# Seven pairs and two single tiles in layer 1: four weight sums read from PSUM while the weight pieces are transposed

## The reference

```python
# layer 0
W  = L0_cond_weights[itok]                      # (32, 64, 64), one 64x64 matrix per batch entry
y  = einsum('bct,bcd->bdt', x, W)
T  = where(abs(w) < 0.05, 0, sign(w)) * mean(abs(w), axis=0)
x  = x + y @ T + b                              # 1024 x 1024
# layer 1
y  = einsum('bct,bcd->bdt', x, L1_cond_weights[itok])
w  = NF4_LEVELS[q_weight] * q_scale             # (1024 out, 1024 in), scale per group of 64
x  = x + y @ w.T + bias + 4 * (y @ lora_A.T) @ lora_B.T
```

## Time and profile before

| what | value |
|---|---|
| time, median of three runs | 360.85 us (360.42 to 361.82) |
| time of the profiled execution | 360.83 us |
| its span, first to last instruction | 359.0 us |
| outside the span | 1.83 us |
| mean granted TensorE clock | 0.998 |
| PE busy | 352.2 us, 98% of the span |

### The profile page before, as it was taken

One profiled execution on the slowest core, in us unless ns is written; L12 is line 12 of the kernel. 1 busy time (PEld: TensorE's weight loads), 2 busy tenths in 40 slices (PEclk: granted clock), 3 DMA queues, 4 the chain that ended last, 5 costly groups with the idle time before them and its releaser, 6 DMA issues.

```text
span 359.0 us, 5496 instructions
## 1 busy us (share of the span) xinstructions
PE 352.2 (98%) x1832; PEld 298.7 (83%) x1832; DVE 242.0 (67%) x363; ACT 161.1 (45%) x285; POOL 224.7 (63%) x146
## 2 busy tenths in 40 slices
PE   8899999999999999999999999999999999999996
PEld 8768788888888888888888888888888888888884
DVE  5789969896996899873899979355262452634523
ACT  2787467776886877752232314213041130321300
POOL 0488999986976888876520220866366663666632
PEclk9999999999999999999999999999999999999999
DMA  6894411953345245333311330304215032150202
GB/s 235 289 328 138 151 31 30 339 203 115 134 168 181 88 156 203 125 120 121 108 76 62 123 118 3 120 0 155 88 63 181 1 140 103 60 182 2 117 31 88
DMA packets 27838, 44.63 MB, mean 124 GB/s; under 512 B 8834, under 2 KB 17026, under 8 KB 27810
## 3 DMA queue, kind: packets, MB, share of 16 engines
q1 hardware_dynamic: 26242, 43.67, 35.0%
q10 hardware_dynamic: 1568, 0.61, 0.7%
HBM read 27.49 MB, written 16.78 MB: 123 GB/s over the span
## 4 chain that ended last, share of the span: by engine, by line
PE 87%; DVE 3%; POOL 2%; issue 2%; ACT 2%; SPq 1%; DMA 1%; POOLq 0%; DVEq 0%; ACTq 0%
PE acc L1157 33%; PE acc L1195 32%; PE xT L1121 10%; PE acc L1137 6%; PE spare L1121 3%; POOL col_scale L596 2%; PE acc L1222 2%; DMA w_in<-in_L_ffn_w 1%; PE acc L1224 1%; DVE hl L872 1%; PE xT L1204 1%; DVE W L925 1%; ACT hh L684 0%; SPq L428 0%; SPq L426 0%
## 5 line engine op out<-in xcount | busy, mean ns | idle before, releaser
L569 POOL TENSOR_TENSOR X<-X,bias 128x1024 f32<-128x1024 f32 x28 | 67.5, 2412 | 29.3 <-PE xT L1121 29.1
L1157 PE MATMUL acc<-T,hh 128*128 128x512 f32 x192 | 76.0, 396 | 0.0
L1157 PE MATMUL acc<-T,hl 128*128 128x512 f32 x192 | 75.0, 391 | 0.0
L723 ACT ACTIVATE spare<-q_raw 128x512 f32<-128x512 int32 x96 | 56.0, 598 | 19.1 <-DVE side_p L913 5.1
L1195 PE MATMUL acc<-W,hh 128*128 128x512 f32 x192 | 61.1, 389 | 0.0
L1021 DVE TENSOR_TENSOR X<-X,acc 128x512 f32<-128x512 f32 x36 | 24.8, 688 | 34.8 <-PE acc L1195 18.6
L1121 PEld LDWEIGHTS xT<-mix,X 128*128 128x128 f32 x352 | 42.7, 192 | 1.5
L1121 PE MATMUL xT<-mix,X 128*128 128x128 f32 x352 | 42.8, 275 | 0.0
L1195 PEld LDWEIGHTS acc<-W,hh 128*128 128x128 f32 x192 | 36.0, 188 | 7.5
L1157 PEld LDWEIGHTS acc<-T,hl 128*128 128x128 f32 x192 | 36.1, 188 | 7.4
L628 POOL TENSOR_TENSOR X<-X,ys 128x512 f32<-128x512 f32 x18 | 22.6, 1286 | 31.1 <-DVE ys L1010 31.1
(11 more groups left out here) (98 smaller groups left out, 662.0 us busy)
## 6 DMA issues: line engine op xcount, KB each, us to landing
out<-X SPq DMA_DIRECT2D x26, 512.0 KB, 3.0
X<-out SPq DMA_DIRECT2D x16, 512.0 KB, 3.4
X<-in_x SPq DMA_DIRECT2D x12, 512.0 KB, 3.4
q_raw<-in_L_ffn_q_weight SPq DMA_DIRECT2D x16, 256.0 KB, 3.0
w_in<-in_L_ffn_w SPq DMA_DIRECT2D x14, 256.0 KB, 6.5
x_first<-in_x SPq DMA_DIRECT2D x4, 512.0 KB, 4.6
out<-x_first SPq DMA_DIRECT2D x4, 512.0 KB, 6.8
out<-X SPq DMA_DIRECT2D x4, 256.0 KB, 2.0
```

The costliest lines, as they stand in the source:

```text
L569: pool.tensor_tensor(x_of(g), x_of(g), (bias1 if g >= NT else bias)[:, :], ALU.add).then_inc(s_xb, 1)
L723: act.activation(dst, q_raw[:, d % QS, :, :].rearrange("p o i -> p (o i)"), ACT.Copy, scale=slope, bias=offset).then_inc(s_line, 1)
L1157: mm = pe.matmul(acc[:, bank_of(q), :], a[:, k, :], b, start=(k == 0 and j == 0), stop=(k == KB - 1 and j == len(terms) - 1))
```

## The change

Layer 1 has two single tiles (16 and 17) and seven pairs. The four sums are no longer made from stored high and low parts. ACT copies a B11 and a B12 piece as they are in PSUM (`keep_block`) ahead of its `high_w`; DVE makes T1, then T3 and T2, then T4 from the bank `wT` and the kept tiles (`sums_with`, one instruction for each sum), directly behind `low_w`. PE's next `turn_w` waits for these too. Pieces except those with `r = 1` are transposed one slot later. The high and low parts of the 16 sums (`high_sum`, `low_sum`: 16 instructions on ACT and 16 on DVE) are made in slots 32 to 35, and the weight tiles lie in another order so that the kept tiles fit. `lines_by` replaces the even share of ACT's lines: in every slot it takes at least the lines that the maxima of the same slot need.

```diff
-    SB = NT + 4
+    SB = NT + 2
-    W_ORDER = (T1, T2, B11, B21, B22, T3, B12)
+    W_ORDER = [(B11, 1), (B12, 1), (B21, 1), (B22, 1), (B11, 0), (B12, 0), (B21, 0), (B22, 0),
+               (T1, 0), (T1, 1), (T2, 0), (T2, 1), (T3, 0), (T3, 1)]
-    NTS = 12
-    COMPLETE = ((T1, 3), (T3, 5), (T2, 6), (T4, 10))
+    SPLIT = (T4, T1, T3, T2)
+    NTS = len(SPLIT)
+    SUMS_BY = (0, 4, 8, 12, NTS * HB)
+    def lines_by(m):
+        done = share(2 * NC * ND, m)
+        if done == 0:
+            return 0
+        d, c = divmod(done - 1, 2 * NC)
+        sign, j = divmod(c, NC)
+        return max(share(2 * NL * ND, m), 2 * NL * d + NL * sign + j + 2)
     def sums_by(m):
-        return NTS * HB * (m - NH * NT) // (NH * (SB - NT))
+        return SUMS_BY[m - NH * NT]
     def turned_in(d):
-        return max(NH * F, ready_in(d) + 2)
+        return max(NH * F, ready_in(d) + 2) + (d % 4 != 1)
...
+            def keep_block(d):
+                j, r = divmod(d, 4)
+                act.wait_ge(s_wT, d + 1)
+                act.activation(as_is((T2, T3)[r], j), wT_flat, ACT.Copy).then_inc(s_asis, 1)
+            def high_sum(u):
+                j, i = divmod(u, NTS)
+                c = SPLIT[i]
+                act.wait_ge(s_made, NTS * HB)
+                if u == 0:
+                    act.wait_ge(s_acc, NH * NT)
+                if c == T2:
+                    act.wait_ge(s_Tl, NTS * j + SPLIT.index(T4) + 1)
+                act.activation(w1(0, c, j), as_is(c, j), ACT.Copy).then_inc(s_Th, 1)
...
                         if turned_in(d) == m - 1:
+                            if d % 4 < 2:
+                                keep_block(d)
                             high_w(d)
...
-                        lines(share(per, m), share(per, m + 1))
+                        lines(lines_by(m), lines_by(m + 1))
...
+            def sums_with(d):
+                j, r = divmod(d, 4)
+                if r == 1:
+                    dve.wait_ge(s_asis, 2 * j + 1)
+                    dve.tensor_tensor(as_is(T1, j), wT_flat, as_is(T2, j), ALU.subtract).then_inc(s_made, 1)
+                elif r == 2:
+                    dve.wait_ge(s_asis, 2 * j + 2)
+                    dve.tensor_tensor(as_is(T3, j), wT_flat, as_is(T3, j), ALU.subtract).then_inc(s_made, 1)
+                    dve.wait_ge(s_made, NTS * j + 1)
+                    dve.tensor_tensor(as_is(T2, j), wT_flat, as_is(T1, j), ALU.subtract).then_inc(s_made, 1)
+                elif r == 3:
+                    dve.wait_ge(s_made, NTS * j + 3)
+                    dve.tensor_tensor(as_is(T4, j), wT_flat, as_is(T2, j), ALU.subtract).then_inc(s_made, 1)
+            def low_sum(u):
+                j, i = divmod(u, NTS)
+                c = SPLIT[i]
+                dve.wait_ge(s_Th, u + 1)
+                dve.tensor_tensor(w1(1, c, j), as_is(c, j), w1(0, c, j).bitcast(F32), ALU.subtract
+                                  ).then_inc(s_Tl, 1)
...
                         if turned_in(d) == m - 1:
                             low_w(d)
+                            sums_with(d)
...
                 if c in SPLIT:
+                    pe.wait_ge(s_Tl, NTS * (HB - 1) + SPLIT.index(c) + 1)
...
                 need(pe, s_Wl, d)
+                need(pe, s_made, NTS * (d // 4) + (0, 0, 1, 3)[d % 4])
```

More of the change, by code:

```diff
@@ L249, in build @@
             x_first = sb("x_first", [P, F, T], F32, first_use)
-        W01 = sb("W01", [P, NPR, 2, HB // 2, BANK], F32R)
+        with ExitStack() as second_use:
+            W01_sums = sb("W01_sums", [P, 2 * NPR, 2, BANK], F32, second_use)
+        W01 = sb("W01", [P, 2 * NPR, 2, BANK], F32R)
         with ExitStack() as first_use:
@@ L257, in build @@
             b_wide = sb("b_wide", [P, KB, P], F32, first_use)
-        W23 = sb("W23", [P, NPR, 2, HB // 2, BANK], F32R)
+        with ExitStack() as second_use:
+            W23_sums = sb("W23_sums", [P, 2 * NPR, 2, BANK], F32, second_use)
+        W23 = sb("W23", [P, 2 * NPR, 2, BANK], F32R)
         def w1(part, c, j):
@@ L263, in w1 @@
                 return W_T4[:, part, j, :]
-            return (W01, W23)[j // 2][:, W_ORDER.index(c), part, j % 2, :]
+            return (W01, W23)[j // 2][:, W_ORDER.index((c, j % 2)), part, :]
         def w_raw(k, n):
@@ L380, in build @@
         s_res1 = sem("s_res1")
-        s_T = sem("s_T")
+        s_asis = sem("s_asis")
+        s_made = sem("s_made")
         s_Th = sem("s_Th")
+        s_Tl = sem("s_Tl")
         def need(eng, s, v):
@@ L398, in tile_done, with as_is @@
             eng.wait_ge(s_res0, F + t + 1 if t < F else NH * (t + 1))
-        def t_plain(c):
-            return plain({T1: 1, T3: 3, T2: 4, T4: 5}[c])
+        def as_is(c, j):
+            return (W01_sums, W23_sums)[j // 2][:, W_ORDER.index((T2 if c == T4 else c, j % 2)),
+                                                0 if c == T4 else 1, :]
         def sum_of(i):
@@ L729, in high_w @@
                     act.wait_ge(s_acc, NH * F)
+                if d == 4:
+                    for t in range(F):
+                        act.wait_ge(s_spill[t], 16)
                 act.activation(w1(0, BLOCK[d % 4], d // 4), wT_flat, ACT.Copy).then_inc(s_Wh, 1)
[L732 to L742, removed]
+            def keep_block(d):
[11 more added lines that the diff above has]
+                act.activation(w1(0, c, j), as_is(c, j), ACT.Copy).then_inc(s_Th, 1)
             def high_A(p, o, h):
@@ L756, in copy_A21 @@
                 if p == 0:
-                    act.wait_ge(s_T, NTS * HB)
+                    act.wait_ge(s_acc, NH * NT)
                 else:
@@ L834, in _ @@
             act.activation(loraA[:, :], a_raw, ACT.Copy).then_inc(s_ah, 1)
-            per = 2 * NL * ND
             for g in range(SB):
@@ L853, in _ @@
                     if g < NT:
-                        lines(share(per, m), share(per, m + 1))
+                        lines(lines_by(m), lines_by(m + 1))
                     else:
-                        high_sums(sums_by(m), sums_by(m + 1))
+                        for u in range(sums_by(m), sums_by(m + 1)):
+                            high_sum(u)
                     if m == NH * F - 2:
@@ L926, in low_w @@
                                   ).then_inc(s_Wl, 1)
[L928 to L970, removed]
@@ L1079, in _ @@
                     else:
-                        sums_of_blocks(sums_by(m), sums_by(m + 1))
+                        for u in range(sums_by(m), sums_by(m + 1)):
+                            low_sum(u)
                     if m == NH * SB - 1:
@@ L1168, in right_ready @@
             def right_ready(c):
-                if c in (T1, T2, T3, T4):
-                    pe.wait_ge(s_T, NTS * (HB - 1) + {T1: 7, T3: 9, T2: 11, T4: 12}[c])
+                if c in SPLIT:
+                    pe.wait_ge(s_Tl, NTS * (HB - 1) + SPLIT.index(c) + 1)
             def bank_left(p, i):
```

## The result

| kernel | median (runs, range) | ratio of changed to before |
|---|---|---|
| before | 360.83 us (6 runs, 360.42 to 361.82) | |
| changed | 362.79 us (6 runs, 362.41 to 363.15) | ratio 1.0053, 95% interval 1.0043 to 1.0063 |

The change makes the kernel slower by 0.53%, 1.96 us, where 362.6 us were forecast with a range of 359.4 to 364.8. The profiled execution took 362.49 us with a span of 360.6; the forecast's sum against the profiled execution of before was 362.58.

What follows compares the result with a forecast made beforehand. The prediction took PE, busy 98% of the span at full clock, to bound the kernel: 360.83 - 2.72 - 0.50 + 4.97 = 362.58, forecast as 362.6 us, with an 8 in 10 range of 359.4 to 364.8.

Steps and rivals of the forecast that it cites:

- The gain, 2.72 us: Layer 1: one pair in place of two single tiles takes 12 matmuls, 2.72 us, off PE, all on the path.
- The place of the loss: Slots 15, 21 and 27: PE waits after pieces 3, 7 and 11, through a blocked line and a next-slot piece.
- The size of the loss, 4.97 us: Layer 0: late transpositions cost PE 1.92 us twice, after pieces 7 and 11, and 1.13 us after piece 3.
- T + 5.58: After pieces 7 and 11: PE goes on at T, wants its next transposition at T + 3.66, gets it then.
- The blocked maxima: Maxima 36, 60 and 84: DVE waits for lines 48, 80 and 112, starting at T + 1.37.
- The 0.50 us given back: Layer 0, piece 10: lines_by gives DVE back about 6 us, and PE the 0.50 us DVE had cost it.
- Sixteen sums at no cost of their own: Layer 0: sixteen sums, 9.6 us of DVE, and eight copies on ACT add nothing to the path by themselves.
- The rule on PSUM reads: New sums read PSUM; about 125 ns overhead against 60 on SBUF would add some 0.2 us; trace doesn't agree.
- All hidden (357.6 us): Rival, layer 0: PE finds the bank read each time, only the gains remain, 357.6 us; chance 0.15.
- DVE as the bound: Rival, layer 0: DVE's share becomes about 5.0 us a slot, its backlog decides, 365 us; chance 0.15.
- PE would wait in the first pair: Layer 1: PE held by the sums at the first pair, some 1 us on top; held for unlikely.
- 362.65: Upper edge of what can't be told from no change; a time above it was given 0.42.

Runs made afterwards that it cites:

- e4: The changed kernel with four single tiles and six pairs, as before the change; 365.26 us, 1.0128 of the kernel before.
- e1: The changed kernel with a fourth buffer for side_p, so a piece's first line waits for piece d - 4; 357.27 us, 0.9908 of before.
- e9: The changed kernel with only pieces 3, 7 and 11 transposed in the slots of the kernel before; 358.46 us, 0.9945 of before.
- e5: The kernel before with lines_by alone; 359.97 us, 0.9976 of before.
- e2: The changed kernel with all pieces transposed in the slots of the kernel before; 357.48 us, 0.9905 of before.
- e3: The kernel before with lines_by and the late transpositions of the changed kernel, no sums in layer 0; 363.61 us, 1.0078 of before.
- e8: The changed kernel with four side_p buffers and T4 computed twice by DVE; 358.78 us, 0.9943 of before.
- e6: The kernel before with two single tiles and seven pairs alone, sums still made in layer 1 from stored parts; 373.59 us, 1.0348 of before.
- e7: The changed kernel with T4 computed twice by DVE, the first into an unused place; 365.92 us, 1.0155 of before.

## Why the prediction was right

**The gain, 2.72 us.** Measured in the profile as 2.70 (windows) and by e4 as 2.5 (medians). The singles take 12.69 us each, the pairs 22.64.

**The place of the loss.** Slots 15, 21 and 27 were named, and there alone PE waits. Both conditions are shown to be needed. e1 takes the blocked line away and leaves the close pairs: no stall. In the changed kernel lines 72 and 104 are blocked too (slots 18 and 24; they are two of ACT's five waits, at 107.41 and 139.13) with no piece to be turned in the next slot: no stall. e9 puts pieces into slots 19 and 25. A stall appears in slot 25, as a maximum of slot 24 needs line 104, and none in slot 19, as no maximum of slot 18 needs line 72.

**The size of the loss, 4.97 us.** Measured 5.13. The chain was computed to end at T + 5.58; at piece 8 T is 116.65 and PE starts at 122.28, T + 5.63. The blocked maxima were put at 87.3, 118.3 and 150.1, and stand at 86.87, 118.06 and 150.06. DVE had 1.3 to 1.5 us in hand there, not 1.4 to 2.1.

**The 0.50 us given back.** Gone as foretold, and somewhat too small: e5 gives 0.8 us for `lines_by` alone, in whose profile the stage is 0.7 us shorter from the last `mixed` before it to the start of tile 16 than before. DVE got back 5.0 us of waits there, where about 6 had been put.

**Sixteen sums at no cost of their own.** Right: e1 and e2 hold them and PE never waits. Where the chain stands, T4 is a link of it and costs what the chain says: 5.13 us of stalls with it, 3.30 without it in e3. It was the step with the least behind it, for e8 shows that 0.6 us more at each T4 would have been felt.

**The rule on PSUM reads** from the Trainium skill (Perfetto Trace Analysis, Optimizing Scalar/DVE Operations) is not borne out here either: the sums that read PSUM take 681 to 682 ns in the mean, the low parts that read SBUF alone 682 where POOL is idle.

**The rivals.** All hidden (357.6 us) did not happen, but it is what the change is worth once the order is mended: e1 and e2 stand at 357.3 and 357.5. DVE as the bound is refuted. The 4.6 and 5.0 us a slot given there for DVE stand in no row; its busy time is 96.97/24 = 4.04 us a slot before and 106.08/24 = 4.42 in e1. That PE would wait in the first pair did not happen; e6 shows what that looks like.

**What was luck.** The sum came within 0.1 us of the profiled execution (362.58 and 362.49) because errors cancelled: the pairs gave 0.02 us less than put, tiles 4 to 15 cost 0.11 more, 0.06 more lies outside the span, and the stage happened to start 0.28 earlier. The mechanism and its size hold without that. On which side of 362.65 the time would fall was chance: the median lies 0.14 above it, the profiled execution 0.16 below, and six runs spread over 0.7 us. That 1.8 us is what can be told from no change was too cautious: the interval of this ratio is 0.1% to each side, and even the interval of e5, 0.24% below, doesn't reach 1.

**What I had not priced** is the clock. It played no part in the changed kernel, where it was full in every slice. It did in e7, 1.65 us, and in e6, where 3.1 us of it stood against a wait that I had put 4.5 us too long: that e6 came near its 375 us was luck too.

The version to keep is e2, one condition less than the changed kernel, or e1: both 0.9% faster than before and 1.5% faster than the changed kernel.

## What to carry to other kernels

When a producer's step is moved later, look up everything that its completion frees, not only who reads its result: here the reader could wait, but the buffer that the transposition frees was wanted by the first instruction of a later piece, and behind that one stood, in order, the very instructions that free the next resource for PE. Write the chain down as times after the moment of release; with durations from the trace it came out within 0.1 us. And when several edits come together, run the cheap ones alone: of this change `lines_by` was a gain and so was the seventh pair with the sums moved, 3.5 us together as e1 shows, and one `+ 1` lost more than that.

## What the runs showed of the hardware

The clock of TensorE can fall after short pauses of PE. In e7 PE's transpositions came about 1.8, 2.6 and 2.6 us late (its idle time is counted as 1.6, 2.4 and 2.4); after the first two it went on at 2.4 GHz, after the third the granted clock was 0.71 over 5 us and `mixed` ran at nearly half speed. In the five timed runs of e7 the mean granted clock was 0.991 to 0.995, and they spread over 2.2 us. In the changed kernel, late by 1.2, 2.0 and 2.0 us, the mean was 0.999 to 1.0. After the 12.46 us of e6 it was 0.50, the 1.2 GHz level, and 12 matmuls took 5.46 us in place of 2.73. The Trainium skill (TensorE: Matmul & The Clock Gate, HAM oscillation) describes the fall after idle gaps of the engine; the rows agree. Why the same pause of 2.6 us brought it once and once not, no run here shows.

DVE's low parts of T4 have two SBUF inputs, and two of the four took longer than the 0.68 us of the others of L979: 2.45 us at 178.43, where POOL ran `add_bias` from 177.93 to 180.33, and 1.26 us at 191.71, where it did from 190.01 to 192.42. The other two, at 183.25 and 195.93 with no POOL instruction beside them, took 0.69. All four lie off the path; that the one causes the other wasn't tried.
